# GELU and the absolute maximum of a tile in one instruction each instead of two halves

## The reference

```python
def act_quant(x):
    scale = 127.0 / jnp.clip(jnp.max(jnp.abs(x), axis=-1, keepdims=True), EPS, None)
    xq = jnp.clip(jnp.round(x * scale), -128.0, 127.0)
    return (xq, scale)

x = x + _L0_xattn_ref(_layernorm(x), ctx_1024, Wq, Wkv, Wout, bout)
h = layernorm(_layernorm(x), gamma, beta)
h = qlinear(h, w1, b1)                    # 512 -> 2048, ternary weights
h = jax.nn.gelu(h, approximate=False)
out = qlinear(h, w2, b2)                  # 2048 -> 512; act_quant needs max|h| of the whole row
x = x + out
```

## Time and profile before

| | |
|---|---|
| median of 3 runs | 541.96 us (541.22 to 542.7) |
| the profiled execution's own time | 543.86 us |
| its span | 542.0 us |
| PE / DVE / ACT / POOL busy | 96% / 83% / 81% / 75% |

### The profile page before, as it was taken

The page is one execution under the profiler, slowest core; times in us unless marked ns, Lnnn a source line. Parts: engine busy times, 40 slices in busy tenths (PEclk is TensorE's granted clock), DMA queues, the critical chain, the costliest instruction groups (busy, mean ns, idle before and its releaser), DMA issues.

```text
span 542.0 us, 8082 instructions
## 1 busy us (share of the span) xinstructions
PE 521.8 (96%) x2387; PEld 226.6 (42%) x2434; DVE 452.4 (83%) x758; ACT 436.8 (81%) x444; POOL 408.4 (75%) x533
## 2 busy tenths in 40 slices
PE   6999789799999999999999999999999999999997
PEld 3443334344444444444444444444444444444443
DVE  1799998999998888888888888889888889877653
ACT  1478988878888888888888888888888888887762
POOL 2099796988998888888898888888888889863300
PEclk8999999999999999999999999999999999999999
DMA  7996834486555545555665446556555554534433
GB/s 271 400 343 217 221 76 106 131 205 161 141 141 142 122 124 120 129 132 138 142 139 125 123 121 142 141 109 138 118 131 132 138 142 103 103 70 98 102 77 97
DMA packets 137014, 78.72 MB, mean 145 GB/s; under 512 B 114245, under 2 KB 114309, under 8 KB 136971
## 3 DMA queue, kind: packets, MB, share of 16 engines
q1 hardware_dynamic: 135819, 76.12, 55.4%
q10 hardware_dynamic: 1152, 2.10, 1.1%
HBM read 33.88 MB, written 17.05 MB: 94 GB/s over the span
## 4 chain that ended last, share of the span: by engine, by line
PE 77%; DVE 3%; issue 2%; ACT 1%; DMA 1%; DVEq 0%; ACTq 0%
PE py L1049 37%; PE p L1034 36%; PE p L1024 3%; DVE hmax L811 1%; DMA hT<-hq 1%; DVE hx L788 1%; DVE hid L805 0%; ACT hid L574 0%; ACT hq L583 0%; DVE xr L834 0%; DVE stat L780 0%; DVE xmax L793 0%; ACT hqT L592 0%; DVE hqT L825 0%; DVE hstep L814 0%
## 5 line engine op out<-in xcount | busy, mean ns | idle before, releaser
L1034 PE MATMUL p<-w1q,xqT 128*128 128x512 bf16 x995 | 229.1, 380 | 3.7 <-issue 1.6
L1049 PE MATMUL py<-w2q,hqT 128*128 128x512 bf16 x1006 | 229.9, 379 | 1.9 <-DVE hqT L825 1.0
L574 ACT ACTIVATE hid<-p,xdeq 128x1024 f32<-128x1024 f32 x128 | 141.8, 1108 | 27.1 <-PE p L1034 17.5
L583 ACT ACTIVATE hq<-hid,hscale 128x2048 int8<-128x2048 f32 x64 | 128.1, 2002 | 42.9 <-DVE hscale L817 42.9
L1049 PEld LDWEIGHTS py<-w2q,hqT 128*128 128x128 bf16 x1024 | 100.1, 98 | 122.1 <-DVE hqT L825 1.5
L1034 PEld LDWEIGHTS p<-w1q,xqT 128*128 128x128 bf16 x1024 | 94.8, 98 | 122.1 <-issue 14.3
L385 POOL TENSOR_TENSOR xr<-xr,attn 128x512 f32<-128x512 f32 x64 | 83.3, 1321 | 19.1 <-DVE attn L723 19.1
L811 DVE TENSOR_REDUCE hmax<-hid 128x1 f32<-128x1025 f32 x64 | 78.1, 1220 | 21.1 <-ACT hid L574 20.7
L400 POOL TENSOR_TENSOR hx<-hx,beta_b 128x512 f32<-128x512 f32 x64 | 91.9, 1456 | 2.0 <-ACT hx L559 2.0
L404 POOL TENSOR_TENSOR xr<-xr,b_b 128x512 f32<-128x512 f32 x64 | 93.0, 1474 | 0.0
L805 DVE TENSOR_REDUCE hid<-hid 128x1 f32<-128x1024 f32 x64 | 77.4, 1210 | 8.9 <-ACT hid L574 8.9
(11 more groups left out here) (86 smaller groups left out, 293.1 us busy)
## 6 DMA issues: line engine op xcount, KB each, us to landing
xr<-x SPq DMA_DIRECT2D x64, 256.0 KB, 2.9
out<-xr SPq DMA_DIRECT2D x64, 256.0 KB, 2.4
raw<-w1T SPq DMA_DIRECT2D x8, 512.0 KB, 11.3
wout<-wout_d ACTq DMA_DIRECT2D x8, 256.0 KB, 8.2
hid<-wvT SPq DMA_DIRECT2D x8, 256.0 KB, 10.0
wout<-w2T SPq DMA_DIRECT2D x3, 512.0 KB, 8.2
xr<-w2T SPq DMA_DIRECT2D x2, 512.0 KB, 6.4
attn<-ctxm_d SPq DMA_DIRECT2D x4, 256.0 KB, 8.5
```

Of the source, the lines that this page charges most:

```text
L574: nc.scalar.activation(hid[:, t % 2, h * HALF:(h + 1) * HALF], p1[:, h * HALF:(h + 1) * HALF], ACT.Gelu, scale=col(xdeq, t)).then_inc(gelu ...
L583: nc.scalar.activation(hq8[:, t % 2, :], hid[:, t % 2, 0:HID], ACT.Copy, scale=col(hscale, t))\
L1034: mm = nc.tensor.matmul(p1[:, n * D:(n + 1) * D], xT[:, k, :], w1q[:, k, n * D:(n + 1) * D], start=False, stop=(k == KD - 1))
L1049: mm = nc.tensor.matmul(py[:, t % 2, :], hqT[:, t % 2, c // 2, c % 2, :], w2q[:, c, :], start=(c == 0), stop=(c == 2 * NJ - 1))
```

## The change

In the loops over s on ScalarE and VectorE, the two GELU instructions of a tile become one over 2048 columns, placed where the second was (behind widen_h), waiting for both halves of the first layer. The two reductions become one over 2048 columns, behind the whole GELU. The tiny steps behind the maximum are the same, moved into a helper. The tiles 0 to 5 of the prologue keep the halves.

```diff
+            def gelu_tile(t):
+                act.wait_ge(xdeq_ready, t + 1)
+                act.wait_ge(hround_done, t - 1)
+                act.wait_ge(ffn1_done, 2 * t + 2)
+                nc.scalar.activation(hid[:, t % 2, 0:HID], p1[:, :], ACT.Gelu, scale=col(xdeq, t)).then_inc(gelu_done, 2)
@@ scalar loop
                 if live(s - 1):
                     round_h(s - 1)
-                if live(s):
-                    gelu(s, 0)
                 if live(s - 2):
                     widen_h(s - 2)
                 if live(s):
-                    gelu(s, 1)
+                    gelu_tile(s)
@@ vector
+                hidden_steps(t)
+
+            def tile_scale(t):
+                dve.wait_ge(gelu_done, 2 * t + 2)
+                nc.vector.tensor_reduce(col(hmax, t), hid[:, t % 2, 0:HID], AX.X, ALU.max,
+                                        apply_absolute_value=True).then_inc(hmax_done, 1)
+                hidden_steps(t)
+
+            def hidden_steps(t):
                 dve.wait_ge(hmax_done, t + 1)
@@ vector loop
                 if live(s):
-                    half_scale(s)
-                    hidden_scale(s)
+                    tile_scale(s)
```

## The result

The changed kernel takes 557.25 us (median of 4 runs, 556.85 to 557.88) beside 542.33 us for the kernel before (4 runs). The ratio is 1.0276, 95% interval 1.0252 to 1.0300: 14.9 us slower. The forecast was 559.8 in a range of 555 to 570, from a difference of 17.8. The profiled execution has a span of 556.1, so its difference to the span of before (542.0) is 14.1; it took 557.88 itself. Three executions at a mean granted clock of 0.56 to 0.85 (one each of the kernel before and of the kernels of experiments 5 and 8) are left out of every median and ratio.

The account below looks back on a forecast made before the run. TensorE bounds the kernel at 7.34 us a tile; the change lengthens the ScalarE-VectorE ring from 6.70 to 7.62, which then sets the period. 57 turns give +18.3, the end returns 0.5: 541.96 + 17.8 = 559.8 us, range 555 to 570.

Parts of the forecast that it names:

- GELU 1.96, maximum 2.29, steps 0.42, round_h 1.90, cast 0.95: Parts of the new ScalarE-VectorE loop per tile, in us; with the 0.10 hand-over they sum to 7.62.
- Hand-over 0.10: Between ScalarE's GELU end and VectorE's maximum start: 0.10 us in each turn.
- The ring: Closed loop of ScalarE and VectorE, one turn per tile: 6.70 us before, 7.62 after, against TensorE's 7.34.
- TensorE waits 0.28 at each bias product: Each tile's bias product needs the previous tile's GELU done, so TensorE waits some 0.28 us there.
- TensorE shows no waits: Sign that would prove the forecast wrong, pointing to rival B.
- The later gate costs nothing: GELU needs the whole first layer, but that is done 1.7 us before ScalarE comes for it.
- VectorE covered, but thinly: VectorE's other work in odd steps ends near 4.6 us after round_h's start, 0.3 before the 4.9 allowed.
- rival A: VectorE arrives late through turns with POOL: maximum up to 0.7 late every other turn, 566 to 580 us; chance 0.13.
- Start level at 112.08: Loop start: round_h(6) at 112.08, exactly where it is in the kernel before, so no gain or loss.
- End 13.4 us after round_h(63): After the loop: round_h(63) at 546.4, last casts, second_layer(63) at 552.7, span end at 559.8.
- B: Rival: GELU and maximum under 3.97 us together, ring within 7.34, TensorE stays the bound; 541 to 543.5 us; chance 0.05.
- C: Rival: merging saves nothing fixed; GELU 2.12, maximum 2.35, ring 7.84, 572 us; 0.06 including anything between it and the forecast.

Follow-up runs that it names:

- experiment 5: Against the kernel before: only ScalarE's widening cast of tile s-2 moved behind both GELU halves; 542.38 us, ratio 0.9995.
- experiment 8: Against the kernel before: the second reduction also rereads 512 columns of the first half (1537 columns, not 1025); 546.3 us, ratio 1.0079.
- 1792 columns: Against the changed kernel: the maximum reads 1792 of the 2048 hidden columns; 542.79 us, ratio to the kernel before 1.0004.
- 1024 columns: Against the changed kernel: the maximum reads only the first 1024 of the 2048 hidden columns; 542.18 us, ratio to the kernel before 0.9995.
- experiment 3: Against the changed kernel: ScalarE's widening cast of tile s-2 moved behind the whole GELU; 543.06 us, ratio to the kernel before 1.0021.
- Experiment 7: Against the changed kernel: the maximum waits on one more, long fulfilled semaphore; 560.93 us, ratio to the kernel before 1.0334.
- experiment 1: Against the changed kernel: GELU in two halves again around the widening cast, maximum still whole; 565.31 us, ratio to the kernel before 1.043.
- 1920-column kernel: Against the changed kernel: the maximum reads 1920 of the 2048 hidden columns; 548.04 us, ratio to the kernel before 1.0105.
- experiment 2: Against the changed kernel: maximum in two halves again, both behind the whole GELU; 567.51 us, ratio to the kernel before 1.048.
- experiment 6: Tile 62's ScalarE cast moved before round_h(63), in step 64 only: changed kernel 557.38 us; with the cast behind GELU in all other steps, 543.08 us.

## Why the prediction was right, point by point

- **TensorE as the floor, 7.34.** Right; the runs with 1792 and 1024 columns and experiment 3 stop there.
- **GELU 1.96, maximum 2.29, steps 0.42, round_h 1.90, cast 0.95.** Measured 1.95, 2.29, 0.42, 1.91, 0.95. The per-column price from neighbouring forms was good to 0.01. (The prediction's 1.06 for 1024 more columns of a reduction doesn't follow from its rows, which give 1.08; the difference is 0.02.)
- **Hand-over 0.10.** Mis-sized: 0.03. I took the 0.09 of rows 3 and 4, where the reduction has two waits; the new one has one. Experiment 7 shows that this is the difference. The ring is 7.545, not 7.62, which is 57 x 0.075 = 4.3 us less.
- **TensorE waits 0.28 at each bias product.** Right in kind, and 0.20 in size, for the same reason. The profile's list of waits hardly names it: between 130 and 520 us it puts 0.9 us in one place down to GELU. The sign "TensorE shows no waits" would have misled; the start times showed the wait.
- **The later gate costs nothing.** Right (1024 columns, ratio 0.9995).
- **VectorE covered, but thinly.** The cast beside POOL's addition ended at 307.91, 1.58 after round_h's start; forecast 1.5. It stayed covered in all turns but one, which cost 0.8. That turn is much as rival A describes, one of 57: the centring starts 0.29 late and takes 1.55 in place of 0.75. What the 0.29 is stays open; the trace names no wait for it, and it stands at the same step in experiment 1's trace. That the two engines take turns was inferred from their times and not tested by a run of its own.
- **Start level at 112.08.** It was 110.18 in this execution, 1.9 earlier. Nearly all of it isn't the change's: round_h(5) began at 102.65 instead of 104.46, and nothing ahead of it was changed. The 1920-column kernel's profiled execution has 104.45 again, that of experiment 3 has 101.22. So the prologue varies by up to 3.2 us between these executions, and a difference of two profiled spans holds that variation too.
- **End 13.4 us after round_h(63).** Wrong step: it was 15.1. I followed the last tile's path and overlooked that tile 62's casts and result(60) stand behind instructions of tile 63, so that TensorE would idle for 2.3 us, and I had its clock stay full. The lower clock after the idle time made second_layer(62) 1.6 us longer, and second_layer(63) had to wait for it.
- **The sum.** Span 559.8 forecast, 556.1 measured: -1.9 from the start (-1.8 prologue, -0.1 first turn), -3.5 from the turns (-4.3 + 0.8), +1.7 at the end. The medians differ by 14.9 where the forecast had 17.8. Part of the closeness is luck: the error at the end had the other sign.
- **Rivals B and C.** C (nothing fixed saved) is what experiments 1 and 2 built, one half each: 0.15 and 0.18 a turn. C's bound of 2.35 for two reductions back to back was too low: they take 2.48 (experiment 2). B (ring under TensorE) is what 1792 columns gave.
- **"The chain will be made of GELU, maximum, round_h and widen_h."** Wrong: the page's chain stays 83% TensorE. TensorE's share near 93% was wrong as well; it shows 96%. The 521.8 us of before over the forecast span give the 93%, but the busy time is 531.1 here, in part because the trace has 47 more matmul records and a slower second layer at the end. The spacing of the bias products and the GELU that never waits showed the ring. Where the turn is a little longer still, the page's chain does show it: ACT has 29% in experiment 7 (turn 7.61), ACT 33% and DVE 27% in experiment 1 (7.69).

## What to carry to other kernels

Before two half instructions are merged, look for the closed loop that they lie in, over all engines and in each engine's queue order, and add up its length without waits; compare that with the period of the busiest engine. Merging saves fixed cost, but it puts in a row what lay side by side. If the loop gets too long, move out of it what doesn't belong there (here a cast of 0.95 us, one place further down the queue): that gave back 14 of the 15 us. And slack in a loop is not free for the taking, since it also absorbs the odd late arrival.

## What the runs showed of the hardware that was not expected

- One more wait on an instruction, on a semaphore that was fulfilled long ago, made the hand-over from another engine 0.07 us slower (1.98 to 2.05 from start to start, experiment 7). Over 57 turns that is 3.9 us; the ratio to the kernel before went from 1.0276 to 1.0334.
- After an idle time of 2.3 us TensorE's granted clock had a mean of 0.67 over the next 5.2 us in the changed kernel's profiled execution. Four more kernels show the same after 2.05 to 2.69 us (0.66 to 0.69), and each time the last two second layers took 8.75 us, not 7.15. In the changed kernel with the move of experiment 6, where TensorE waited 0.66 and 1.57 us, the clock stayed 1.00.
